# Copying v over the key rows: matrix products on TensorE replaced by transfers through DRAM

## The reference, cut to what matters

```python
w = jnp.exp(-jnp.exp(time_decay + jnp.tanh(x5[:, :, 1] @ decay_w1) @ decay_w2))
r = (x5[:, :, 3] @ Wr.T).reshape(b, l, H, S)
k = (x5[:, :, 0] @ Wk.T).reshape(b, l, H, S)
v = (x5[:, :, 2] @ Wv.T).reshape(b, l, H, S)
def step(s, rkvw):
    r_t, k_t, v_t, w_t = rkvw
    a = k_t[:, :, :, None] * v_t[:, :, None, :]
    out = jnp.einsum('bhk,bhkd->bhd', r_t, u * a + s)
    return (a + w_t[:, :, :, None] * s, out)
```

## Time and profile before

| What | us |
|---|---|
| median of the 3 runs | 2303.19 (2302.08 to 2303.35) |
| the profiled execution | 2301.0 |
| its span, first to last instruction | 2299.2 |
| PE busy in the span | 2141.9 |
| DVE busy | 1952.8 |
| ACT busy | 1260.4 |
| POOL busy | 585.2 |

### The profile page before, as it was taken

How to read it: one execution, slowest core, us unless ns; L and a number is a source line. 1 busy time by engine, 2 the same in 40 slices (tenths; PEclk the granted TensorE clock), 3 DMA queues, 4 the chain that set the end, 5 groups by cost and what they waited for, 6 DMA issues and landing times. The chain is left out here.

```text
span 2299.2 us, 41734 instructions
## 1 busy us (share of the span) xinstructions
PE 2141.9 (93%) x14176; PEld 1477.2 (64%) x14176; DVE 1952.8 (85%) x4863; ACT 1260.4 (55%) x4405; POOL 585.2 (25%) x700
## 2 busy tenths in 40 slices
PE   3698799999999999999999999999999999999866
PEld 2475576767666676767667676766767676666533
DVE  0258898989899898989989898999989899998982
ACT  1736374573838466383746648373755738374312
POOL 1131314222331422232141322224141222314200
PEclk7799899999999999999999999999999999999977
DMA  7100101001010100001010100101010010100000
GB/s 268 35 7 20 31 11 49 11 11 41 11 50 11 49 11 31 21 11 50 11 49 11 48 3 11 50 11 50 11 49 1 11 50 11 50 2 29 1 19 10
DMA packets 48978, 69.88 MB, mean 30 GB/s; under 512 B 20512, under 2 KB 26656, under 8 KB 48768
## 3 DMA queue, kind: packets, MB, share of 16 engines
q1 hardware_dynamic: 48768, 67.21, 8.9%
HBM read 50.42 MB, written 16.78 MB: 29 GB/s over the span
## 5 line engine op out<-in xcount | busy, mean ns | idle before, releaser
L1226 DVE TENSOR_TENSOR_SCAN st<-ws,st 128x256 f32<-128x256 f32 x1024 | 637.4, 686 | 0.1
L862 ACT ACTIVATE probs_or_mixes<-probs_or_mixes,least 128x128 f32<-128x128 f32 x1024 | 398.9, 403 | 117.4 <-DVE least L1173 116.3
L1215 DVE TENSOR_TENSOR st<-bank_pair,kT 128x1016 f32<-128x1016 f32 x256 | 308.0, 1203 | 88.0 <-PE bank_pair L717 88.0
L1236 DVE TENSOR_TENSOR st<-st,rT 128x1024 f32<-128x1024 f32 x256 | 317.9, 1243 | 0.0
L1173 DVE CUSTOM_DVE_ANT_0 probs_or_mixes<-bank,nmask 128x128 f32<-128x128 f32 x1024 | 231.1, 285 | 100.5 <-PE bank L566 76.0
L1108 POOL TENSOR_SCALAR rstd<-rstd 128x1 f32<-128x1 f32 x96 | 26.5, 276 | 1098.4 <-ACT cin L895 600.1
L1102 POOL TENSOR_TENSOR probs_or_mixes<-probs_or_mixes 128x512 f32<-128x512 f32 x160 | 190.1, 1218 | 341.4 <-DVE probs_or_mixes L1267 341.4
L862 ACT ACTIVATION_READ_ACCUMULATOR probs_or_mixes<-probs_or_mixes,least 128x1 f32 x1024 | 206.4, 202 | 0.0
L717 PE MATMUL bank_pair<-v_hi,sel 32*128 32x256 f32 x1024 | 193.8, 339 | 10.9 <-DVE st L1215 10.6
L717 PE MATMUL bank_pair<-v_lo,sel 32*128 32x256 f32 x1024 | 166.6, 286 | 0.0
L717 PEld LDWEIGHTS bank_pair<-v_hi,sel 32*128 32x128 f32 x1024 | 114.5, 185 | 72.3 <-issue 35.4
(11 more groups left out here) (150 smaller groups left out, 4216.3 us busy)
## 6 DMA issues: line engine op xcount, KB each, us to landing
inputs_turned<-in_ctx_turned SPq DMA_DIRECT2D x16, 512.0 KB, 3.6
inputs_turned<-in_x_turned SPq DMA_DIRECT2D x16, 512.0 KB, 4.6
xin<-in_x SPq DMA_DIRECT2D x16, 512.0 KB, 3.7
x<-xin SPq DMA_DIRECT2D x16, 512.0 KB, 4.1
keep<-x SPq DMA_DIRECT2D x16, 512.0 KB, 3.6
out<-keep SPq DMA_DIRECT2D x32, 256.0 KB, 2.0
wo<-in_wo SPq DMA_DIRECT2D x2, 1024.0 KB, 11.3
nmask<-in_mask SPq DMA_DIRECT2D x16, 128.0 KB, 4.1
```

Source lines behind the costliest of these rows:

```text
L862: last = fn(pr[:, n % 4, j, :], pr[:, n % 4, j, :], ACT.Exp, bias=least[:, n, j:j + 1], scale=-1.0, accum_out=rsum[:, n, j:j + 1])
L1215: tt(dst, src, over(kv, DU, 1), ALU.mult).then_inc(outer.sem, 1)
L1226: last = nc.vector.tensor_tensor_scan(v, ws[:, c].rearrange("p b t -> p (b t)"), v, 0.0, ALU.mult, ALU.add)
L1236: tt(v, v, over(rT[:, u // PER, :], DU, 1), ALU.mult).then_inc(weighed.sem, 1)
```

## The change

- `spread` leaves PE. v is one float32 tile, `vT`, written by ACT alone; v_hi, v_lo, the DVE step proj_v, POOL's sum for dg and bank_pair are gone. DVE's `readout` multiplies by vT instead of dg.
- New on SP: `save_v.p` writes two chunks of vT to the DRAM tensor `v_rows` with four transfers of 64 KB; `spread.u` reads eight rows of 4 KB from it, each sixteen times, into a slot of `st` (512 KB). It waits for the save and for `summed`, which frees the slot.
- `outer` now multiplies the slot in place by k. It and `first` wait for the transfer (`v_there`).
- `st` has five slots instead of four, with a pitch of 1028 floats; the transfer writes from the second float on.
- The ring has six banks (0, 1, 2, 4, 5, 6).
- All five orders are new, and SP has one of its own (`SP_ORDER`) in place of `turn`.
- The order of value columns in a chunk changes, and constants and offsets with it; the amount of work there does not.

```diff
-SLOTS = 4
+SLOTS = 5
+PITCH = DU * T + 4
 PE_ORDER = """
-reduce.4+2 spread.12+2 low_rank.0+1 spread.13+2 key.0 reduce.5+2 tdecay.0+1 spread.14+2 low_rank.2+1 proj_r.0+1
+reduce.4+2 reduce.5+2 low_rank.0+1 key.0 low_rank.2+1 tdecay.0+1 proj_r.0+1 proj_v.0+1 proj_k.0+1 decay.0+1 decay.1+1
...
 ACT_ORDER = """
-state.0+1 state.1+1 key.0 first.14+2 tdecay.0+1 proj_v.0+1 decay.0+1 first.15+2 proj_r.0+1 first.0+1 proj_k.0+1
+key.0 proj_r.0+1 tdecay.0+1 first.13+2 first.14+2 state.0+1 first.15+2 proj_v.0+1 decay.0+1 decay.1+1 proj_k.0+1
...
 DVE_ORDER = """
-outer.12+2 mix.0+1 mix.1+1 outer.13+2 scan.12+2 mix.2+1 mix.3+1 outer.14+2 readout.2+2 weigh.12+2 outer.15+2
+weigh.12+2 mix.2+1 mix.3+1 outer.13+2 outer.14+2 readout.2+2 outer.15+2 scan.13+2 scan.14+2 scan.15+2 weigh.13+2
...
+SP_ORDER = """
+load_m.0 spread.9+2 spread.10+2 spread.11+2 spread.12+2 load_c.0 load_s.2+1 save.0+1 load_x.0 load_t.0 store.0+3
+spread.13+2 spread.14+2 spread.15+2 bring.0+2 load_s.3+1 save_v.0+1 spread.0+1 spread.1+1 spread.2+1 spread.3+1
+spread.4+1 load_s.0 spread.5+1 spread.6+1 spread.7+1 save_v.1+1 spread.8+1 load_s.1
+"""
-RING, READOUT = [0, 1, 2, 4], 7
+RING, READOUT = [0, 1, 2, 4, 5, 6], 7
+        def slot(g, u):
+            return (UNITS * g + u) % SLOTS
+        def v_there(eng, g, u):
+            eng.wait_ge(landed[slot(g, u)], ((UNITS * g + u) // SLOTS + 1) * 16)
+            def save_v(g, p):
+                wait(sp, outer.sem, outer.after(g - 1, 2 * PER * (p + 1)))
+                key = ("proj_v", p)
+                sp.wait_ge(emptied[XB.of(key)], XB.through(key, g))
+                for c in (2 * p, 2 * p + 1):
+                    for half in range(2):
+                        sp.dma_start(v_rows[c, :, half].rearrange("m (k t) -> m k t", k=2),
+                                     vT[64 * half:64 * half + 64, c, :]).then_inc(v_saved[p].sem, 16)
+            def spread(g, u):
+                c, p = u // PER, u // (2 * PER)
+                sp.wait_ge(v_saved[p].sem, v_saved[p].after(g, 4))
+                wait(sp, summed.sem, summed.after(g, (u - SLOTS) // 2 + 1))
+                r = HC * (UNIT_D[u % PER][0] // 2)
+                src = v_rows[c, r:r + HC].rearrange("h s n -> h (s n)")
+                n = slot(g, u)
+                sp.dma_start(st[:, n, 1:DU * T + 1],
+                             src.unsqueeze(1).to_broadcast([HC, HD, DU * T])).then_inc(landed[n], 16)
-            def spread(g, u):
-                wait(pe, outer.sem, outer.after(g, u))
-                for k in range(2):
-                    for part in (v_hi, v_lo):
-                        for s in range(2):
-                            last = mm(pair[:, s, k * T:(k + 1) * T], sel[r, d % 4, :], part[r, c, :],
-                                      start=part is v_hi, stop=part is v_lo)
-                last.then_inc(spreaded.sem, 1)
@@ r_times_k, on POOL
-                tt(dg[:, c % 2, :], v_hi[:, c, :].bitcast(F32), v_lo[:, c, :].bitcast(F32),
-                   ALU.add).then_inc(v_joined.sem, 1)
@@ outer_, on DVE
-                wait(dve, summed.sem, summed.after(g, (u - SLOTS) // 2 + 1))
-                dve.wait_ge(spreaded.sem, spreaded.after(g, u + 1))
-                dst = st[:, u % SLOTS, :].rearrange("p (d b t) -> p d b t", d=DU, b=NB)[:, :, :, 1:]
-                src = pair[:].rearrange("p s (k b t) -> p (s k) b t", k=2, b=NB)[:, :, :, 0:L - 1]
+                v_there(dve, g, u)
+                dst = st[:, slot(g, u), 0:DU * T].rearrange("p (d b t) -> p d b t", d=DU, b=NB)[:, :, :, 1:]
-                tt(dst, src, over(kv, DU, 1), ALU.mult).then_inc(outer.sem, 1)
+                tt(dst, dst, over(kv, DU, 1), ALU.mult).then_inc(outer.sem, 1)
@@ readout, on DVE
-                tt(dg[:, c % 2, :], ps[:, T:2 * T], dg[:, c % 2, :], ALU.mult).then_inc(diag.sem, 1)
+                tt(dg[:, c % 2, :], ps[:, T:2 * T], vT[:, c, :], ALU.mult).then_inc(diag.sem, 1)
@@ proj_v, on DVE
-                tt(v_lo[:, both, :], ps[:].rearrange("p (c n) -> p c n", c=2), v_hi[:, both, :].bitcast(F32),
-                   ALU.subtract).then_inc(free, 1)
```

197 lines of the change are left out of this document (81 added, 116 removed).

## The result

The changed kernel takes 2376.97 us (median of 4 runs, 2371.07 to 2379.02) and the kernel before, beside it on the same chip, 2302.64. The ratio is 1.032, with an interval of 1.030 to 1.034. It is slower by 74 us where the prediction said 127 us faster, and it lies outside the range.

The account below looks back on a forecast made before the run. PE was taken as the bound before, DVE after at 122.4 us; with 0.5 and 0.8 for waits, 123.7 an iteration. 114.3 + 249.5 + 13 x 123.7 + 200 = 2171.9, plus 4.0: 2176 us, range 2146 to 2225.

Parts of the forecast that it names:

- What leaves PE: Sixteen spreads an iteration leave PE, 0.6 us each, 9.6 in all; PE then needs 121.3 us.
- What DVE needs: DVE's work in a steady iteration: 122.4 us after the change, making it the bound, PE 1.1 below.
- I add 0.4 (bounds 0, and 5.6 ...): DVE's outers slowed beside POOL's adds: +0.4 us an iteration, besides +0.6 for outer reading and writing the slot.
- POOL counted at nothing: POOL's sum for dg, 4 x 0.72 us, goes; counted at nothing, since POOL idles most of the time.
- What the transfers cost: SP's copies into slots: 2.4 us of data each, landing 4.8 after issue; bounds on landing 3.6 and 5.2.
- its loop: Loop reduce.0, copy 5, outer.5, mixes, POOL, proj_v: 117 us plus 4.8 landing, 121.8; sets the iteration from landing 5.4.
- the second rival: Copies at half rate, 3.2 us of data each, third copy 2.5 late: 125.7 an iteration, 2202 us; chance 0.20.
- The tightest place: Copies 13 to 15 behind `out<-keep`: the third lands 0.5 us late for outer.15, adding 0.5 (0 to 2.5).
- The rival on the orders: New orders don't fit, ACT waiting for copies in `first`: 4 to 5 us an iteration, 2232 us; chance 0.10.
- The two engines together: PE and DVE both near their limit, so small misses no longer vanish: +0.8 us an iteration.
- The signs: Right: shift starts 123 to 124.5 us apart, DVE over 97% busy. Wrong in kind: above 132 with DMA share above half.
- That rival: Copies fill the queue, deciding from 7.5 us of data each; at 9 us, 157 an iteration, some 2620; chance 0.07.

Follow-up runs that it names:

- cut copies: The changed kernel with each of the 16 copies an iteration cut to 16 of 1024 elements in a row: 2286.4 us.
- the pair with five banks: The changed kernel with copies cut to 16 elements a row and a ring of five banks, outer reading PSUM or in place: 2325.7 and 2411.4 us.
- the version whose waits are filled: The changed kernel with copies reading 16 rows, proj_k.0 ahead of proj_v.0, ffn_v.0 ahead of turn_n and `first` behind the norms: 2270.6 us.
- The run on the kernel before: The kernel before with outer multiplying the slot in place, PE still spreading and waited for: 2362.5 us, 59 more.
- the run whose outer reads PSUM: The changed kernel with copies cut to 16 elements a row, ring of five banks, outer's first operand from an otherwise unused PSUM bank: 2325.7 us.

## Why the prediction was wrong, step by step

By the medians, 90.6 of the 201 us between forecast and result are the transfers' (the changed kernel less the one with cut copies). 110 are left. The contention takes 52 to 86 of them, if it is worth here what it is in the kernel before or in the pair with five banks. 25 to 58 us are then open.

The stages say where they lie. In the run with cut copies whose profile stands at the median, the first two iterations take 250.3 us and the end 198.5, against 249.5 and 200 forecast. So these two parts were right but for the copies, and what is not the copies' lies in the steady iterations, 132.3 us where 123.7 was forecast.

- **What leaves PE** was right. Its 121.3 us are 122.7 busy in the version whose waits are filled (1594.6 / 13, at a granted clock of 0.99). In the changed kernel PE is busy 125.1 us for the same products at a granted clock of 0.96, which falls behind its waits. I had forecast it full.
- **What DVE needs** is the first step that failed. "I add 0.4 (bounds 0, and 5.6 ...)": DVE is busy 126.0 us an iteration in the changed kernel where 122.4 was forecast, so with the 0.4 this term is 4.0, and it is 4.8 in the pair. The bounds held both, and I took the lower end, though the earlier trace rows had a weigh at 1.57 us beside POOL. Most of it is outers: their mean is 1.39 over the steady part where 1.24 was priced, some 2.4 us for sixteen. The rest is mostly scans, which the prediction did not price: 0.712 us against 0.684, 64 of them an iteration, 1.8 us. The row for one outer was read (weigh at 1.24) and was right for an outer alone, with a median of 1.21. The rest of the arithmetic was right: with the operand in PSUM, DVE is busy 121.7 where the sum without its two terms for outer is 121.4.
- **POOL counted at nothing.** "POOL idles most of the time" is true and says nothing of its eight additions, which PE waits for. They grew from 1.22 to 1.45 us, and proj_v's wait from about nothing to 2.8. Contention was priced on one of its two engines only, and as DVE's busy time only. The run on the kernel before shows what that misses: it cost 3.8 us an iteration on a kernel whose DVE had 9.9 to spare.
- **What the transfers cost** is the second step that failed, by size. I took 2.4 us of data a copy with 3.2 as the end; copies in a row land 4.3 apart. Eight engines at the rate of the earlier trace rows would be 2.4, so the number of engines alone was covered, and the repeated rows were not. The sum's own warning, that no transfer before reads a row sixteen times, was used for the lower end and not for the upper. The landing, 6.9 us after the issue for a copy alone and 10.3 in the median, passed the 4.8 taken and the 5.4 that the prediction set for its loop. The 4.8 was also added up wrongly: a load's 3.6 less its 1.6 of data, with 2.4 of data in place, is 4.4, and at half rate it is 5.2, not the 5.8 that the second rival has for its loop. These slips are worth 0.4 us in a wait, 5 us in all.
- **The tightest place** was named wrong. Outers 14 and 15 do wait, 0.36 and 1.47 us in the rows above, within the bounds of 0 to 2.5, and DVE waits 4.0 us an iteration for copies in all. The larger loss is at copies 9 to 12, where not DVE but ACT waits for them, ahead of the norms, 9.6 us in the iteration shown (2.22, 3.95, 2.31 and 1.09). The rival on the orders had that mechanism, "ACT now waits for copies in `first`", with 0.10 and 4 to 5 us. Moving those steps gave 3.9 an iteration. It failed as a rival of its own: with early copies the order costs nothing, so it belonged to the slow copies and should have been added to them.
- **The two engines together**, 0.8 us, was too little. In the run with cut copies PE waits 7.8 us and DVE 4.8 an iteration, with neither full. PE's 2.8 at proj_v are for POOL's additions, and 0.8 in the run whose outer reads PSUM, so contention in POOL's chains has a part in it. How what is left over divides between such waits, the new orders and the slower clock, no run tells.
- **The signs** named in the prediction were the right ones: outer at 1.38 in place of 1.22 to 1.25, ACT waiting for copies with PE waiting for ACT, PE waits over 8 us, shift starts over 132 apart. PE waits over 8 us were to mean "wrong in kind", and it was. The shift starts were to mean it "with the DMA share above a half"; the share is 0.36. The queue was never full, and the slow case needed no full queue. That rival was priced for one mechanism, and two terms, one well up in its bounds and one beyond them, did it together.

## What to carry to other kernels

An operand that moves from PSUM to SBUF changes what its instruction shares with GpSimd: price both sides, the instruction itself and GpSimd's work beside it, and follow who waits for GpSimd, however idle it is. A broadcast out of memory by one transfer was slow here for two reasons, an outermost extent of 8 and rows that are read again and again; take its time from a row with the same shape or bound it generously. When a wait for such a copy appears on an engine that works in order, look at what stands behind the waiting step: with `first` behind the norms the same late copies cost 52 us less.
